# Linear attention in a fused two-layer network: plain f32 products against three products of high and low halves

## The reference, cut to what matters

```python
q = relu(x @ Wq.T + bq); k = relu(x @ Wk.T + bk); v = x @ Wv.T + bv     # 16 heads of 16
kv    = einsum('bnhd,bnhp->bhdp', k, v)
denom = maximum(einsum('bnhd,bhd->bnh', q, k.sum(axis=1)), 1e-6)
y = einsum('bnhd,bhdp->bnhp', q, kv) / denom + x
return (y - mean(y)) / sqrt(var(y) + 1e-5) * gamma + beta
```

## Time and the profile before

| | |
|---|---|
| median of three runs | 2080.39 us (2079.14 to 2080.5) |
| span of the profiled execution | 2078.5 us |
| mean granted TensorE clock | 0.998 |
| PE busy | 2031.0 us, 98% of the span |
| DVE busy | 1206.5 us, 58% |
| ACT busy | 1123.6 us, 54% |
| POOL busy | 497.8 us, 24% |
| stage `linear_feed` | from 843.4 to 1044.5 us of the span |
| L339 (queries) | 32 instructions, 14.6 us busy |
| L348 (keys and values) | 64 instructions, 31.3 us busy |

### The profile page before, as it was taken

How to read it: one execution, slowest core, us unless ns; L and a number is a source line. 1 busy time by engine, 2 the same in 40 slices (tenths; PEclk the granted TensorE clock), 3 DMA queues, 4 the chain that set the end, 5 groups by cost and what they waited for, 6 DMA issues and landing times. The chain is left out here.

```text
span 2078.5 us, 46348 instructions
## 1 busy us (share of the span) xinstructions
PE 2031.0 (98%) x18825; PEld 1819.9 (88%) x18825; DVE 1206.5 (58%) x3626; ACT 1123.6 (54%) x2556; POOL 497.8 (24%) x411
## 2 busy tenths in 40 slices
PE   7999999999999999899899999999999999999998
PEld 7999999999999999477768888788999999999998
DVE  6756565656565655567668898735939724233311
ACT  5556565655565656333268777644444444444443
POOL 1000020000000000123311222144444444444444
PEclk9999999999999999999999999999999999999999
DMA  4000200000000000100031110101010101101000
GB/s 152 22 17 22 77 22 17 22 17 22 17 22 16 22 17 2 46 1 1 1 99 33 32 33 23 42 1 34 28 41 1 41 1 41 41 1 41 1 11 31
DMA packets 48786, 57.81 MB, mean 28 GB/s; under 512 B 6528, under 2 KB 40128, under 8 KB 48448
## 3 DMA queue, kind: packets, MB, share of 16 engines
q1 hardware_dynamic: 48576, 54.85, 8.2%
HBM read 46.72 MB, written 2.10 MB: 23 GB/s over the span
## 5 line engine op out<-in xcount | busy, mean ns | idle before, releaser
L963 POOL TENSOR_TENSOR right_h<-right_hr,right_h 128x512 fp32r<-128x512 f32 x256 | 341.3, 1333 | 418.1 <-ACT right_hr L1285 418.1
L1284 ACT ACTIVATE right_h<-bank,dec_b 128x512 fp32r<-128x512 f32 x256 | 176.2, 688 | 390.1 <-PE bank L83 364.3
L83 PE MATMUL bank<-lat_wv,lat_kv_t 128*128 128x256 f32 (+1 forms) x1728 | 259.0, 300 | 0.7 <-issue 0.7
L83 PE MATMUL bank<-lat_kv_t,lat_qk 128*128 128x320 f32 x1536 | 254.7, 315 | 0.0
L83 PEld LDWEIGHTS bank<-lat_kv_t,lat_qk 128*128 128x128 f32 x1536 | 226.3, 188 | 7.7
L2255 ACT ACTIVATE lat_p<-bank,lat_neg_max 128x320 f32<-128x320 f32 x256 | 136.2, 532 | 173.8 <-DVE lat_neg_max L2379 173.8
L83 PEld LDWEIGHTS bank<-lat_wv,lat_kv_t 128*128 128x128 f32 x1728 | 223.0, 190 | 6.8 <-issue 1.1
L83 PE MATMUL bank<-dec_xt,dec_lo 128*128 128x512 f32 x512 | 200.5, 392 | 0.0
L1285 ACT ACTIVATE right_hr<-bank,dec_b 128x512 f32<-128x512 f32 x256 | 174.5, 682 | 0.0
L1768 POOL TENSOR_TENSOR lat_rs_rstdc<-lat_rs_varc,lat_rs_halfc 128x4 f32<-128x4 f32 x16 | 16.2, 1015 | 635.0 <-DVE lat_rs_varc L1760 635.0
L1132 PE MATMUL bank<-dec_hi,right_h 128*128 128x256 f32 x1024 | 161.5, 279 | 1.2 <-POOL right_h L963 1.2
(11 more groups left out here) (327 smaller groups left out, 3914.7 us busy)
## 6 DMA issues: line engine op xcount, KB each, us to landing
raw_w<-in_L_ffn_W SPq DMA_DIRECT2D x16, 1024.0 KB, 6.5
lat_ctx_raw<-in_ctx SPq DMA_DIRECT2D x16, 512.0 KB, 4.1
right_ctx_raw<-in_ctx_turned SPq DMA_DIRECT2D x16, 512.0 KB, 3.7
lat_kv_t<-lat_lt SPq DMA_DIRECT2D x32, 128.0 KB, 2.1
out_x<-x_sb SPq DMA_DIRECT2D x4, 512.0 KB, 2.9
x_sb<-in_x SPq DMA_DIRECT2D x1, 1792.0 KB, 14.6
lat_xl_now<-lat_xl SPq DMA_DIRECT2D x7, 256.0 KB, 4.6
ahead_room<-in_L_xattn_Wq SPq DMA_DIRECT2D x1, 1024.0 KB, 6.9
```

The costliest lines, as they stand in the source:

```text
L83: mm = pe.matmul(out, lhs(a, k), rhs(b, k), start=first and k == 0 and n == 0, stop=last and k == KD - 1 and n == 2)
L963: pool.tensor_tensor(h[:, g % 2, 1, :], hr[:, g % 2, :], h[:, g % 2, 0, :].bitcast(F32), ALU.subtract).then_inc(h_lo, 1)
L1284: act.activation(h[:, n % 2, 0, :], h_bank[n % 2][:, :], ACT.Relu, bias=bias).then_inc(h_hi, 1)
```

## The change

`xt` gets a high and a low half in fp32r. ACT still writes the high half (L494). A new DVE function `rows_low` writes the low half from the PSUM bank, two 128x512 instructions a chunk: for chunk 0 between the high halves of `wgu` and `wd`, for the others right after `norm_y.close` and ahead of the last `hidden` of the loop. The weights are split too: DVE makes the high halves of `wq` (128x512) and `wkv` (128x1024) as the first things of the stage, POOL makes the low halves before its first `add_beta`. They live in rooms that the decoder's operands take later (`near.wk` and `near.ctx_t[:, 1]`), and so the work of `near_split` is dealt out anew. `queries` and `keys_values` call `product3` (six fp32r matmuls an output) and wait for the low halves.

```diff
-        xt = tools.sb("xt", [P, KD, CH])
+        xt = tools.sb("xt", [P, 2, KD, CH], F32R)
+        wq_s, wkv_s = near.wk, near.ctx_t[:, 1]
...
+            pool.wait_ge(wl_hi, 1)
+            pool.tensor_tensor(wq_s[:, 1], wq[:, :, :], wq_s[:, 0].bitcast(F32), ALU.subtract).then_inc(wl_lo, 1)
+            pool.wait_ge(wl_hi, 2)
+            pool.tensor_tensor(wkv_s[:, 1], wkv[:, :, :], wkv_s[:, 0].bitcast(F32), ALU.subtract).then_inc(wl_lo, 1)
             pool.wait_ge(loads, 64)
             add_beta(0)
...
             def queries(c):
-                pe.wait_ge(l_xt, 2 * c + 2)
+                pe.wait_ge(l_lo, 2 * c + 2)
+                if c == 0:
+                    pe.wait_ge(wl_lo, 1)
                 for m in range(KD):
-                    for kd in range(KD):
-                        mm = pe.matmul(st_bank[m][:, :], wq[:, kd, m * P:(m + 1) * P], xt[:, kd, :],
-                                       start=kd == 0, stop=kd == KD - 1)
-                    mm.then_inc(q_psum, 1)
+                    product3(pe, st_bank[m][:, :], lambda a, kd: wq_s[:, a, kd, m * P:(m + 1) * P],
+                             lambda a, kd: xt[:, a, kd, :]).then_inc(q_psum, 1)
 
             def keys_values(t):
                 i = t % PER
-                if t >= 1:
+                if t == 0:
+                    pe.wait_ge(wl_lo, 2)
+                else:
                     pe.wait_ge(v_ready, t)
-                for kd in range(KD):
-                    mm = pe.matmul(kv_bank[:, :], xt[:, kd, i * P:(i + 1) * P], wkv[:, kd, :],
-                                   start=kd == 0, stop=kd == KD - 1)
-                mm.then_inc(kv_psum, 1)
+                product3(pe, kv_bank[:, :], lambda a, kd: xt[:, a, kd, i * P:(i + 1) * P],
+                         lambda a, kd: wkv_s[:, a, kd, :]).then_inc(kv_psum, 1)
...
+            def rows_low(c):
+                for half in range(2):
+                    dve.wait_ge(l_xt, 2 * c + half + 1)
+                    cols = lambda a: xt[:, a, :, half * 2 * P:(half + 1) * 2 * P]
+                    dve.tensor_tensor(cols(1), st_bank[half][:, :].rearrange("p (k n) -> p k n", k=KD),
+                                      cols(0).bitcast(F32), ALU.subtract).then_inc(l_lo, 1)
...
                 if (c, i) == (1, 1):
                     dve.wait_ge(near_in, 112)
+                    dve.tensor_copy(near.ctx_t[:, 0, 0], near.ctx_raw[:, 0]).then_inc(near_hi, 1)
+                if (c, i) == (2, 1):
+                    dve.wait_ge(near_hi, 1)
+                    dve.tensor_tensor(near.ctx_t[:, 0, 1], near.ctx_raw[:, 0], near.ctx_t[:, 0, 0].bitcast(F32),
+                                      ALU.subtract).then_inc(near_lo, 1)
+                if (c, i) == (3, 1):
+                    dve.wait_ge(q_psum, KD * NCH)
                     for g, dst in enumerate((near.wk, near.wv)):
                         dve.tensor_copy(dst[:, 0], kv_raw[:, g]).then_inc(near_hi, 1)
-                if (c, i) == (1, 2):
-                    dve.wait_ge(near_hi, 2)
+                if (c, i) == (3, 2):
+                    dve.wait_ge(near_hi, 3)
                     for g, dst in enumerate((near.wk, near.wv)):
                         dve.tensor_tensor(dst[:, 1], kv_raw[:, g], dst[:, 0].bitcast(F32), ALU.subtract).then_inc(near_lo, 1)
...
+            dve.tensor_copy(wq_s[:, 0], wq[:, :, :]).then_inc(wl_hi, 1)
+            dve.tensor_copy(wkv_s[:, 0], wkv[:, :, :]).then_inc(wl_hi, 1)
             for kd in range(KD):
                 dve.tensor_copy(wgu[:, 0, kd], wf[:, kd]).then_inc(gu_hi, 1)
+            rows_low(0)
             dve.tensor_copy(wd[:, 0], wdf).then_inc(wd_hi, 1)
...
                     if i == PER:
                         norm_y.close(dve, c)
+                if c + 1 < NCH:
+                    rows_low(c + 1)
                 if c >= 1:
                     hidden(c - 1, NH - 1)
```

More of the change, by code:

```diff
@@ L240, in linear_feed @@
         l_shift, f_shift, l_xn, l_psum, l_xt = sem("l_shift"), sem("f_shift"), sem("l_xn"), sem("l_psum"), sem("l_xt")
+        l_lo, wl_hi, wl_lo = sem("l_lo"), sem("wl_hi"), sem("wl_lo")
         q_psum, q_done, kv_psum = sem("q_psum"), sem("q_done"), sem("kv_psum")
@@ L493, in rows_turned @@
                     act.wait_ge(l_psum, 2 * c + half + 1)
-                    act.copy(xt[:, :, half * 2 * P:(half + 1) * 2 * P],
+                    act.copy(xt[:, 0, :, half * 2 * P:(half + 1) * 2 * P],
                              st_bank[half][:, :].rearrange("p (k n) -> p k n", k=KD)).then_inc(l_xt, 1)
```

## The result

The changed kernel takes 2086.96 us (median of 7 runs), the kernel before 2080.39: ratio 1.0031, 95% interval 1.0021 to 1.0041, so 6.6 us slower. One of the seven runs took 5036.26 us, for no known reason, and is left out of the ratio; the other six lie between 2085.91 and 2087.06 us. The forecast was 2084.0 with a range of 2079.8 to 2087.3, so the time lies inside it, 0.3 us from its upper end. The profiled execution has a span of 2085.0 us against 2078.5.

The account below looks back on a forecast made before the run. It took a DVE-TensorE-ACT chain to bound chunk 0, and TensorE, with DVE close behind, chunks 1 to 3; 3.5 + 1.0 - 1.1 + 0.15 - 0.9 + 0.6 + 0.35 = +3.6 on 2080.4 gave 2084.0 us, 80% range 2079.8 to 2087.3.

Parts of the forecast that it names:

- start of the stage: Before tile 0's keys: DVE's displaced train costs 1.2 us and POOL's add_beta turn 2.3, together +3.5 us.
- chunk 0, loop: Chunk 0's tiles: shorter products give back three times 0.35 us, -1.1, against +1.0 for TensorE's clock.
- chunk 0, end: End of chunk 0: rows_low(1) goes mostly into DVE's wait for POOL's power, +0.15 us; later queries stay hidden.
- chunk 1: Chunk 1: three products in the loop give 1.05 us, the delayed end takes 0.15, in all -0.9 us.
- chunk 2: Chunk 2: DVE has no idle time, so near_split and rows_low(3) cost +0.6 us; bounds -1.4 and +1.3.
- chunk 3 and rest: Chunk 3: DVE's moved casts and subtractions bring tile 15's contexts 0.35 us later; bounds -1.05 and +1.2.
- What one product gains: Queries, keys and values: each output gains 0.35 us from fp32r matmuls; three passes for four would give 0.43.
- TensorE's clock, +1.0: After TensorE's idle time before the first states: 3.4 us at half speed cost 1.0 us; bounds 0 and 3.
- third rival: The clock costs more, two half-speed stretches or POOL's low halves hitting DVE's train: +2 to +4, 2087 us; chance 0.20.
- `rows_low` at the chunks' ends: Ends of chunks 1 and 2: rows_low ahead of hidden delays turn_ffn, counted as +0.15 and about +0.35 us.
- `near_split`: Loops of chunks 2 and 3: moved subtractions load a DVE without slack, +0.25 and +0.35 us.
- likeliest case: The forecast itself, all terms as summed: 2084.0 us, own range 2082.3 to 2085.7; chance 0.50.

Follow-up runs that it names:

- e1: The changed kernel plus unread matmuls in TensorE's two long idle times of chunk 0 (five and three): span 2081.4 us.
- e6: The kernel before plus three unread matmuls in TensorE's idle time at the end of chunk 3: median not distinguishable from the kernel before.
- e10: The changed kernel plus three unread matmuls in TensorE's idle time at the end of chunk 3: 1.67 us gained there; runs up to 2086.99 us.
- e2: The changed kernel with POOL's first add_beta waiting until DVE has written the wd low half: span 2082.1 us, runs 2080.84 to 2085.83.
- e7: The changed kernel with DVE making the wq and wkv low halves, and only one wgu low before tile 0's keys: span 2079.5 us, ratio 1.0001.
- e12: The changed kernel with e7's start, e8's order altered, dummies in chunks 0 and 3, and the second wgu low waiting for shift_f: median 2077.04 us, ratio 0.9985.
- e4: The changed kernel without rows_low in chunks 1 to 3, whose products reuse chunk 0's low half: span 2083.3 us.
- e5: The changed kernel with all its splits and waits, but the plain f32 matmuls of before: span 2092.3 us.
- e8: The changed kernel with near_split dealt out by DVE's idle time, wv and context halves in chunk 1, wk in chunk 3: span 2083.3 us.
- e3: The kernel before with only the change's new places of near_split: span 2081.3 us.

## Why the prediction was right in kind, and too small

By its own steps, the distances of the changed kernel less those of the kernel before:

```
                              forecast   measured   of it the clock
start of the stage               +3.5       +3.10
chunk 0, loop (-1.1 and 1.0)     -0.1       +0.92     +1.87 (e1)
chunk 0, end                    +0.15       +1.25     +1.23 (e1)
chunk 1                          -0.9       -1.06
chunk 2                          +0.6       +0.45
chunk 3 and rest                +0.35       +1.62     +1.01 (e6, e10)
sum                              +3.6       +6.28
```

- **What one product gains**: 0.35 us was right. Chunk 1's loop, with three products and no other limit, is 0.97 us shorter, 0.32 each, and nearer to the 0.35 of the rows than to the 0.43 of the four-pass count.
- **The start**: both parts stand, at 1.0 and 2.09 us for 1.2 and 2.3 (e2), and e7 took them both away. How it came about differs: I had `add_beta` take its turn behind the `wd` cast and hold a `wgu` low, and looked only at DVE instructions that read SBUF twice. But `add_beta` was first, by 0.17 us, and the cast was held. The size came out nearly the same, 2.09 us for the 2.3 reckoned for another instruction; in e12 `add_beta` held a subtraction for as long (3.89 us in place of 1.75). So the size was right, and the order of the two was not. The Trainium skill (SBUF — State Buffer, Who interferes with whom) has this lock, won by whoever issues first and held for the whole instruction, and counts `cast` among the operations that can take the shared ports; this trace agrees, 3.03 us for 0.94.
- **TensorE's clock, +1.0**: the forecast had it fall once, behind the first wait. This is the term of the sum that was mis-sized, and it is the forecast's own third rival, the clock at 1.2 GHz for more than one stretch, that came true. It measured 1.87 us in chunk 0's loop, where it was low for 6.8 us and not 3.4. It came back at the end of chunk 0, where I had TensorE's later queries hidden: I looked at the 3 us of idle time as free, and so it was, but not the half speed behind it. And it cost 1.0 us more at the end of chunk 3, behind an idle time of 3.49 us that hadn't changed. Together 4.1 and not 1.0.
- **Chunk 0's loop without the clock**: -0.95 (13.16 against 14.11), for -1.1.
- **`rows_low` at the chunks' ends**: I charged 0.15 and 0.35; measured -0.09 and +0.13, and e4 shows no cost at all. That is since the queries behind it are 0.7 us shorter: with plain products (e5) the same two ends took 0.65 and 0.87 us more than in the kernel before.
- **`near_split`**: DVE's limit in chunks 2 and 3 was the right mechanism: +0.32 and +0.45 in the loops for +0.25 and +0.35, and 1.0 and 1.2 us against what the loops can do (e8).
- **The cases**: 2086.96 lies beside the third rival's 2087 and outside the likeliest case's own range of 2082.3 to 2085.7; the side was slower, to which I gave 0.37 against 0.60 for no measurable change. What separates the two is the clock: without it the sum would be 2.2 us measured for 2.6 forecast. That the time still fell inside the range is owed to this rival, whose middle is the range's upper end, and not to the sum.

Open: what decides whether the clock falls behind an idle time of some 3 us, and for how long. It isn't the kernel alone, since runs of e2 and of e10 differ among themselves, while all of the six runs of the changed kernel from 2085.91 to 2087.06 us have a granted clock of 0.995 or 0.996, so that its loss is no chance of one trace. The 6.8 us at the end of chunk 3 came in e3 too, with `near_split` moved and nothing else; whether by DVE's order or because that place lies 1.5 us later is not shown.

## What to carry to other kernels

A cheaper product pays only if the splits that feed it fit the idle time of the engine that makes them, in that place; count the whole train that lies behind the new waiting instruction, and look on the other engine for instructions that read SBUF at the same moment. A wait of about 3 us on TensorE isn't only its own length, as chunk 0 shows (1.87 and 1.23 us): price the work behind it at half speed too, and fill it with matmuls that nobody reads where that costs nothing. Here the same edit went from 6.6 us slower to 3.4 us faster without one product changed (2.5 against the kernel before with its own dummies).

## What the runs showed of the hardware that wasn't expected

- The same idle time ends differently. Behind 3.09 us before the queries of chunk 1 twelve matmuls took 4.59 us in the changed kernel and 3.07 in e10. Behind 3.49 us at the end of chunk 3 the clock was low for 3.4 us in the kernel before and for 6.8 in the changed one. Executions of one kernel differ too: ten runs of e2 have mean granted clocks from 0.993 to 0.998 and times from 2080.84 to 2085.83 us.
- It can fall behind less: after 2.19 us of idle time in e2's chunk 0 it was low for 3.4 us.
- The low clock can begin inside the idle time: at 857.7 in the changed kernel, 1.6 us before TensorE resumed.
- A POOL instruction of four columns took 1.26 us and not 0.20 behind a DVE subtraction of 1536 columns; and a DVE cast with one SBUF input was held as well, 3.03 us for 0.94 beside `add_beta`.
